# Moving two kinds of elementwise work from GpSimd to VectorE in the opening stage of a graph network, and reordering its loads

## The reference

```python
h = einsum('bnf,of->bno', x, W_w) + W_b;  h[:, 0, :] = 0
mask = adj[1:, :] > 0
neigh = einsum('ji,bjf->bif', mask, h[:, :N-1, :])
s = einsum('bif,fi->bi', h, a[:64]) + einsum('bif,fi->bi', neigh, a[64:]);  s[:, 0] = 0
h_prime = s[:, :, None] * h.sum(axis=1)[:, None, :]
x = layernorm(x + leaky_relu(h_prime, 0.01))
x = layernorm(x + attention_layers(x, ...))     # 32 + 8 attention instances, most of the time
```

## Time and profile before

| | before |
|---|---|
| median of 3 runs | 3126.8 us (3121.39 to 3129.04) |
| profiled execution, its own time | 3127.07 us |
| its span in the trace | 3125.3 us |
| TensorE busy, share of the span | 94% |
| VectorE busy | 86% |
| ScalarE busy | 73% |
| GpSimd busy | 83% |
| mean granted TensorE clock | 0.974 of full speed |

### The profile page before, as it was taken

The page is one execution under the profiler, slowest core; times in us unless marked ns, Lnnn a source line. Parts: engine busy times, 40 slices in busy tenths (PEclk is TensorE's granted clock), DMA queues, the critical chain, the costliest instruction groups (busy, mean ns, idle before and its releaser), DMA issues. The chain is left out here.

```text
span 3125.3 us, 124905 instructions
## 1 busy us (share of the span) xinstructions
PE 2923.1 (94%) x49770; PEld 2168.0 (69%) x49770; DVE 2681.5 (86%) x5523; ACT 2275.4 (73%) x2654; POOL 2587.7 (83%) x1458
## 2 busy tenths in 40 slices
PE   7957999999999999999999999999998889999990
PEld 5435777777777777777777777777776867777760
DVE  6966888888888888988889888988897579999988
ACT  1267777777777777777777777777776567777773
POOL 4465999998898999999999989999999079888882
PEclk8979999999999999999999999999999999999995
DMA  6139899889999889998899898898987878898773
GB/s 245 48 132 342 146 167 165 157 155 161 159 166 163 157 158 168 165 165 158 157 171 165 166 150 160 164 164 168 160 158 144 294 152 158 163 165 163 155 140 89
DMA packets 1443985, 514.30 MB, mean 165 GB/s; under 512 B 1359503, under 2 KB 1417293, under 8 KB 1441357
## 3 DMA queue, kind: packets, MB, share of 16 engines
q1 hardware_dynamic: 1443532, 507.36, 82.7%
HBM read 105.30 MB, written 66.06 MB: 55 GB/s over the span
## 5 line engine op out<-in xcount | busy, mean ns | idle before, releaser
L583 POOL TENSOR_TENSOR low<-probs 128x1024 f16<-128x1024 f32 x1280 | 2395.7, 1893 | 358.3 <-ACT probs L870 255.0
L870 ACT ACTIVATE probs<-scores,shifted_max 128x2048 f32<-128x2048 f32 x640 | 1282.5, 2004 | 223.6 <-DVE shifted_max L1077 219.9
L736 PE MATMUL ps<-operands 128*128 128x512 f16 x2560 | 973.7, 380 | 7.9 <-DMA v_parts<-h_d 5.8
L737 PE MATMUL ps<-operands 128*128 128x512 f16 x2560 | 972.2, 380 | 0.0
L1072 DVE CUSTOM_DVE_ANT_0 scores<-ps,mask,neg_max 128x1024 f32<-128x1024 f32 x640 | 821.6, 1284 | 126.4 <-issue 73.3
L898 ACT COPY probsT<-ps 128x1024 bf16<-128x1024 bf16 x640 | 647.6, 1012 | 374.7 <-PE ps L745 374.7
L745 PEld LDWEIGHTS ps<-ident,probs 128*128 128x128 bf16 x10240 | 650.1, 98 | 370.0 <-issue 202.3
L1072 DVE CUSTOM_DVE_ANT_0 scores<-ps,mask 128x1024 f32<-128x1024 f32 x640 | 781.3, 1221 | 134.1 <-PE ps L737 124.0
L745 PE MATMUL ps<-ident,probs 128*128 128x128 bf16 x10240 | 780.5, 219 | 9.9 <-DVE probsT L1086 6.9
L756 PE MATMUL ps<-v_parts,probsT 128*128 128x64 f16 x10240 | 685.4, 193 | 5.5 <-issue 5.5
L755 PE MATMUL ps<-v_parts,probsT 128*128 128x64 f16 x10240 | 685.0, 193 | 1.4 <-DVE outs L1136 1.4
(11 more groups left out here) (156 smaller groups left out, 1734.7 us busy)
## 6 DMA issues: line engine op xcount, KB each, us to landing
operands<-hT_d SPq DMA_DIRECT2D x40, 512.0 KB, 4.3
operands<-hT_d SPq DMA_DIRECT2D x80, 256.0 KB, 4.0
v_parts<-h_d SPq DMA_DIRECT2D x40, 512.0 KB, 4.9
probsT<-low SPq DMA_TRANSPOSE x1280, 3.5
z_d<-outs SPq DMA_DIRECT2D x38, 512.0 KB, 3.9
h_d<-probs SPq DMA_DIRECT2D x32, 512.0 KB, 5.9
hT_d<-probsT SPq DMA_DIRECT2D x32, 512.0 KB, 5.3
scores<-z_d SPq DMA_DIRECT2D x32, 512.0 KB, 4.9
```

Source lines behind the costliest of these rows:

```text
L583: pool.tensor_tensor(low[:, u, w], probs[:, u, w], high[:, u, w], ALU.subtract).then_inc(sem(f"low{half}"), 1)
L736: pe.matmul(ps[:, b, :], hi_lo[:, p, t * P:(t + 1) * P], hi_lo[:, p, w], start=True, stop=False)
L737: scored = pe.matmul(ps[:, b, :], hi_lo[:, p, t * P:(t + 1) * P], lo_hi[:, p, w], start=False, stop=True)
L870: act.activation(probs[:, 1 - u, :], scores[:, 1 - u, :], ACT.Exp, bias=shifted_max[:, 1 - u:2 - u], scale=-1.0, accum_out=row_sum[:, held ...
```

## The change

The 16 remainders and the 16 own-node products move from GpSimd to VectorE. A remainder becomes one instruction that also zeroes node 0 (x times node_on minus the upper half), so the memset of tile 0 is gone. VectorE's loop now does for each tile: two remainders (one ahead of the mask's need), the mask, the product, and its sum. Remainder 0 and mask 0 are made before VectorE splits the weights.

The loads are reordered: the first weight, its doubled copy and a come first, then x in four DMAs of 1 MB (four node tiles of all batches each), with the adjacency tiles and the other weights between them. The one semaphore of the weights becomes four. TensorE's 123 idle transposes become two float32 matmuls of 512 columns, and the multiplication of a now comes before the turning of the other weights. ScalarE makes upper halves 0 to 3 before it copies the turned a, the others behind it.

```diff
+            sp.dma_start(w_nat[0:D, 0:D], w0).then_inc(sem("w0_loaded"), 16)
+            sp.wait_ge(sem("twice_cleared"), 1)
+            for k in range(2):
+                sp.dma_start(w0_twice[k * D:(k + 1) * D, k * D:(k + 1) * D], w0).then_inc(sem("w0_loaded"), 16)
+                sp.dma_start(w0_twice[k * D:(k + 1) * D, P + k:P + k + 1], b0.rearrange("(c o) -> c o", o=1)).then_inc(sem("w0_loaded"), 16)
+            sp.dma_start(a_in, a).then_inc(sem("a_loaded"), 16)
+            def load_x(q):
+                w = slice(q * G * D, (q + 1) * G * D)
+                sp.dma_start(xs[:, :].rearrange("p (b n) -> p b n", b=B)[:, :, w],
+                             x.rearrange("b (p t) c -> p b (t c)", t=NT)[:, :, w]).then_inc(sem(f"x_loaded{q}"), 16)
+            load_x(0)
+            load_adj(0)
             (weights wh and wo: "weights_loaded")
+            load_x(1)
+            load_adj(1)
             (bh and the four rows: "rows_loaded")
+            load_x(2)
+            load_adj(2)
+            load_x(3)
...
-            for k in range(NT):
-                pool.wait_ge(sem(f"x_loaded{k // 8}"), 16 * B)
-                pool.wait_ge(sem("hi_made"), k + 1)
-                remainder = pool.tensor_tensor(pair(col(h_lo, k, BD)), x_btc[:, :, k, :], pair(col(h_hi, k, BD)), ALU.subtract)
...
-            pool.wait_ge(sem("a_copied"), 4)
-            for k in range(NT):
-                since(pool, sem("s1_made"), k - 1)
-                pool.tensor_tensor(pair(work[:, k % 2, :]), x_btc[:, :, k, :], aT[:, k:k + 1, 0:D].to_broadcast([P, B, D]),
-                                   ALU.mult).then_inc(sem("s1_prod"), 1)
...
-            for _ in range(123):
-                pe.transpose(banks16(7, 1)[:, 0:P], ident_h[:, :], ident_h[:, :])
-            pe.wait_ge(sem("weights_loaded"), 16 * 13)
+            for _ in range(2):
+                pe.matmul(ps[:, 7, :].rearrange("p (o n) -> p o n", o=4), ident[:, :], ident[:, :].rearrange("p (o n) -> p o n", o=1).to_broadcast([P, 4, P]),
+                          start=True, stop=True)
+            pe.wait_ge(sem("w0_loaded"), 16 * 5)
             pe.transpose(ps[0:D, 0, 0:D], w_nat[0:D, 0:D], ident[0:D, 0:D])
+            pe.wait_ge(sem("a_loaded"), 16)
             (the 32 matmuls on a, then wait for "weights_loaded" and the six other turns)
...
+            high_x(0)
             act.wait_ge(sem("a_turned"), 1)
             (four copies of aT, one of c12)
-            high_x(0)
-            high_x(1)
+            for q in range(1, 4):
+                high_x(q)
...
+            def low_x(k):
+                dve.wait_ge(sem(f"x_loaded{k // 4}"), 16)
+                dve.wait_ge(sem("hi_made"), k + 1)
+                dve.scalar_tensor_tensor(pair(col(h_lo, k, BD)), x_btc[:, :, k, :], node_on[:, k:k + 1], pair(col(h_hi, k, BD)),
+                                         ALU.mult, ALU.subtract).then_inc(sem("lo_made"), 1)
+            dve.wait_ge(sem("pool_const"), 7)
+            low_x(0)
+            make_mask(0)
             (the splitting of the weights, L949 to L961)
+            dve.wait_ge(sem("a_copied"), 4)
             for k in range(NT):
+                if k:
+                    for j in (2 * k - 1, 2 * k):
+                        if j < NT:
+                            low_x(j)
+                    make_mask(k)
+                v = work[:, k % 2, :]
+                dve.tensor_tensor(pair(v), x_btc[:, :, k, :], aT[:, k:k + 1, 0:D].to_broadcast([P, B, D]), ALU.mult).then_inc(sem("s1_prod"), 1)
+                dve.wait_ge(sem("s1_prod"), k + 1)
+                dve.tensor_reduce(s1[:, k, :], pair(v), AX.X, ALU.add).then_inc(sem("s1_made"), 1)
```

More of the change, by code:

```diff
@@ L344, in _ @@
             load_x(0)
-            for k in range(3):
-                load_adj(k)
+            load_adj(0)
+            sp.dma_start(w_nat[:, D:3 * D].rearrange("p (k c) -> p k c", k=2),
+                         wh.rearrange("(k h) d c -> (h d) k c", k=2)).then_inc(sem("weights_loaded"), 16)
+            sp.dma_start(w_nat[0:D, 3 * D:7 * D], wo).then_inc(sem("weights_loaded"), 16)
             load_x(1)
+            load_adj(1)
+            sp.dma_start(bh_rows[:, :, :].rearrange("p h d -> p (h d)"),
+                         bh.rearrange("h d -> (h d)").rearrange("(o n) -> o n", o=1).to_broadcast([P, H * D])).then_inc(sem("rows_loaded"), 16)
+            for k, row in enumerate((b0, bo, gamma, beta)):
+                sp.dma_start(rows[:, k, :], row.rearrange("(o c) -> o c", o=1).to_broadcast([P, D])).then_inc(sem("rows_loaded"), 16)
+            load_x(2)
+            load_adj(2)
+            load_x(3)
             for k in range(3, NT):
@@ L603, in _ @@
             pe.wait_ge(sem("pool_const"), 7)
-            for _ in range(123):
-                pe.transpose(banks16(7, 1)[:, 0:P], ident_h[:, :], ident_h[:, :])
-            pe.wait_ge(sem("weights_loaded"), 16 * 13)
+            for _ in range(2):
+                pe.matmul(ps[:, 7, :].rearrange("p (o n) -> p o n", o=4), ident[:, :], ident[:, :].rearrange("p (o n) -> p o n", o=1).to_broadcast([P, 4, P]),
+                          start=True, stop=True)
+            pe.wait_ge(sem("w0_loaded"), 16 * 5)
             pe.transpose(ps[0:D, 0, 0:D], w_nat[0:D, 0:D], ident[0:D, 0:D])
+            pe.wait_ge(sem("a_loaded"), 16)
+            for t in range(NT):
+                a_t = a_in.rearrange("f (p t) -> f t p", t=NT)[:, t, :]
+                pe.matmul(ps[:, 2 + t // 4, t % 4 * P:(t % 4 + 1) * P], a_t, w0_twice[:, 0:P], start=True, stop=True)
+                turned = pe.matmul(ps[:, 6, 2 * t:2 * t + 2], a_t, w0_twice[:, P:P + 2], start=True, stop=True)
+            turned.then_inc(sem("a_turned"), 1)
+            pe.wait_ge(sem("weights_loaded"), 16 * 2)
             for k in range(2):
@@ L613, in _ @@
             last.then_inc(sem("weights_turned"), 1)
[L615 to L619, removed]
             pe.wait_ge(sem("weights_copied"), 2)
@@ L802, in _, with high_x @@
             act.wait_ge(sem("pool_const"), 7)
-            def high_x(half):
-                act.wait_ge(sem(f"x_loaded{half}"), 16 * B)
-                for k in range(half * 8, half * 8 + 8):
+            def high_x(q):
+                act.wait_ge(sem(f"x_loaded{q}"), 16)
+                for k in range(4 * q, 4 * q + 4):
                     act.activation(pair(col(h_hi, k, BD)), x_btc[:, :, k, :], ACT.Copy, scale=node_on[:, k:k + 1]).then_inc(sem("hi_made"), 1)
+            high_x(0)
             act.wait_ge(sem("a_turned"), 1)
@@ L947, in _, with make_mask @@
         def _(dve):
-            dve.wait_ge(sem("weights_loaded"), 16 * 13)
+            def low_x(k):
[3 more added lines that the diff above has]
+                                         ALU.mult, ALU.subtract).then_inc(sem("lo_made"), 1)
+            def make_mask(k):
+                dve.wait_ge(sem(f"adj_loaded{k % 3}"), k // 3 * 16 + 16)
+                dve.tensor_scalar(col(mask, adj_tile(k), N).rearrange("p (t q) -> p t q", t=NT),
+                                  adj_slots[k % 3].rearrange("p (q t) -> p t q", t=NT), 0.0, None, ALU.is_gt).then_inc(sem("mask_made"), 1)
+            dve.wait_ge(sem("pool_const"), 7)
+            low_x(0)
+            make_mask(0)
             dve.wait_ge(sem("weights_turned"), 1)
@@ L962, in _ @@
             b0_all = rows[:, 0:1, :].to_broadcast([P, B, D])
+            dve.wait_ge(sem("a_copied"), 4)
             for k in range(NT):
[L964 to L970, removed]
+                if k:
[7 more added lines that the diff above has]
+                dve.tensor_reduce(s1[:, k, :], pair(v), AX.X, ALU.add).then_inc(sem("s1_made"), 1)
+            dve.wait_ge(sem("rows_loaded"), 16 * 5)
             dve.wait_ge(sem("degree_ready"), 1)
```

## The result

The changed kernel takes 3185.84 us (median of 4 runs, 3182.86 to 3188.56) against 3127.92 us (4 runs, 3121.39 to 3131.74): ratio 1.0185, 95% interval 1.0169 to 1.02. It is 58 us slower, where 12 us faster was forecast. The span went from 3125.3 to 3181.5 us.

A forecast was written before the change was run, and what follows sets the result against it. It took the path to L973 through TensorE's sum loop as the bound: 10.4 us from the start plus 6.3 from stall and clock, less 4.8 for VectorE's pace, gives 11.9 less, 3115 us; range 3106.5 to 3121.

The forecast's parts named there:

- L973: VectorE's step after TensorE's last neighbour sum: forecast to start at 90.3 instead of 102.26 us, 11.9 us less.
- prediction's own sign of being wrong: Wrong if the first sum matmul lies far from 29 us, or the time behind L973 is not 3023 us.
- C: TensorE's sum loop: pauses before tiles 2 to 8 keep the clock at half, 32 us late, 3159; chance 0.04.
- Start of the sums: TensorE's neighbour-sum loop was to start at 29.1 us instead of 39.5, 10.4 us earlier.
- the half clock: TensorE's matmuls on a were to take 14.05 us again if the clock is again at half.
- rival A: TensorE's matmuls on a at full clock take 7 us instead of 14: 19.3 us less, 3107.5; chance 0.21.
- The two float32 matmuls ahead: TensorE's opening, before the work on a: about half of 7 us, done at 6.7, hidden behind the load.
- VectorE's tile: VectorE's loop: two remainders 1.32, mask 1.80, product and sum 1.36, together 4.48 us, longer than TensorE's 3.62.
- 6.3 us of stall and clock: TensorE's sum loop: 6.3 us gained from the mask stall and the lowered clock, less 4.8 for VectorE's pace.

The follow-up runs named there:

- after_pad119: The changed kernel with 119 unused transposes added to TensorE's list between the last neighbour sum and the first projection; 3114.14 us, ratio 0.9959 to the kernel before.
- after_less9: The changed kernel with 23 instead of 32 idle transposes right before the first attention loop; 3116.14 us, ratio 0.9984 to the kernel before.

## Why the prediction was wrong

The prediction failed in one step, the last sentence of its first paragraph: "What comes after has the same instructions in the same order, so whatever L973 gains or loses, the end gains or loses." The instructions were the same, their places in TensorE's list were not. I counted the 123 transposes as time, and taking them out also moved all behind them by 238 instructions. What the runs show in place of that step is a branch of 3.6 instead of 0.36 us in 14 turns of the first attention loop, 70.2 us in all with what follows from it. The prediction's own sign of being wrong caught it: 3023 us were to lie behind L973, and 3092 do. No rival held this mechanism; C, the slower one, had another place and another reason and ended at 3159. The range to 3121 left it out altogether, as it left out C.

Point by point, the steps in front of it:

- **L973.** Forecast 90.3, measured 89.54. after_pad119 with the step repaired: 3114.14 against the 3115 forecast. The closeness is in part luck. Of the 12.7 us at L973 only 9.9 are left at the first branch of the attention loop (549.7 against 559.6), so the gain does not pass through unchanged as the sentence has it; after_less9, repaired without an added instruction, is 5.6 us below before; and executions of the kernel before spread from 3114 to 3137 us over the sessions.
- **Start of the sums.** Forecast 29.1, measured 28.34: a was issued at 3.92 (4.0) and worked on from 9.05 (9.5). The 32 float32 matmuls took 14.05 us again (9.05 to 23.10), as in the sum. The reason given there, the half clock, and with it rival A, do not hold. The trace of the changed kernel has no clock record before 33.3 us (a window there shows 1.00 for that reason alone). after_pad119 has the same opening and has one. The granted clock is 1.00 from 7.6 to 11.0 and 0.50 from there to 31.5, and the pairs that start at 9.03 and 9.92, at the full level, take 0.89 and 0.87 us like the others (the windows' columns are as in the earlier trace rows):

```profile
9.03 0.70 PE L599 MATMUL ps<-scratch,v_parts 128*128 128x128 f32 x2 [1.78 <-DMA v_parts<-in_L_gnn_a]
9.92 0.68 PE L599 MATMUL ps<-scratch,v_parts 128*128 128x128 f32 x2
10.79 0.78 PE L599 MATMUL ps<-scratch,v_parts 128*128 128x128 f32 x2
11.66 0.78 PE L599 MATMUL ps<-scratch,v_parts 128*128 128x128 f32 x2
```

```profile
9.00:11.00 2.00, 1.97 (x9) 1.97 (x10) 0.00 (x0) 0.00 (x0) 0.00 (x0) 1.00 1.09 379
12.00:22.60 10.60, 10.60 (x50) 10.60 (x50) 2.55 (x2) 3.84 (x5) 0.00 (x0) 0.50 0.85 300
```

By these two pairs A's 7 us were out of reach whatever the clock, and 14.05 came out right for another reason than the one given. What does set this pace is open. Rival A also read the clock's fall in the earlier trace rows as 2.9 us behind the last transpose; a mean of 0.62 in the window from 15 puts it at 15.24, which is 2.5 us.
- **The two float32 matmuls ahead.** Forecast 3.5, measured 3.78 us, behind them 1.8 us of idleness before a is there.
- **VectorE's tile.** Forecast 4.48, measured 4.44. The two remainders take 1.32 us from start to start (51.86 to 53.18) and the mask 1.80 (to 54.98), both as forecast; product and sum take 1.32 instead of 1.36. The masks last 1.88 to 1.91, never longer. TensorE waited for masks in front of tiles 4 to 7, 0.67 us each, where 0.8 us in front of tiles 2 to 8 were forecast.
- **Adding up of the parts.** Not priced by the prediction in this way: the loads alone brought 15.9 us at L973 (102.26 to 86.36), the move alone 4.8, both 12.7. On top of the new loads the move costs 3.2 us, since the GpSimd work there no longer starves a mask. I had put 6.3 us of stall and clock to the move's credit in any order of loads.

## What to carry to other kernels

Before costing any edit at nothing behind its own stage, count the instructions it adds or removes ahead of a large loop on each engine, TensorE's dummies too, and look at the duration of the loop's branch in the trace of before and after: 0.36 against 3.6 us tells it in one row. Where it is dear, a few instructions more or fewer in front of the loop are a cheap repair; here nine transposes fewer gave 64 to 70 us. And price a stall by contention in the new order of things, not in the old one.

## What the runs showed that I had not expected

- A branch hint is at the loop's start in all kernels (31 to 40 ns), and still the branch costs 0.36 or 3.6 us by its place: 18 instructions decided (188 against 206).
- A dear branch ends 1.4 us after a 16 KB instruction packet has landed, and the place decides how late that packet starts: at 206 it starts 1.0 to 1.3 us after the branch in the changed kernel.
- A float32 pair of the work on a takes 0.87 to 0.89 us at either level of the granted clock.
- A 3.6 us stall costs 5.0 us a turn, since TensorE's clock falls to 0.50 for 3.4 or 6.8 us at 13 of the 14.
- The same pair of mask and GpSimd work either takes turns (2.1 us a GpSimd instruction, masks up to 2.90) or leaves one mask waiting for some 19 us.
